# A grouped convolution whose three tap blocks are multiplied last to first

## The reference

```python
x = x + conv1d(x, W0, taps=9, groups=4, pad=4) + ctx0 + side     # layer 0
x = x + einsum(agg_w1[b], x) + agg_b1                            # layer 1, one 128x128 matrix per batch
x = x + einsum(agg_w2[b], x) + agg_b2                            # layer 2, likewise
x = x + conv1d(x, W3, taps=9, groups=4, pad=4) + ctx3 + side     # layer 3
# agg_w[b] = sum over 8 experts of softmax(mlp(cond[b])) * expert weight
```

## Time and profile before

| | |
|---|---|
| profiled execution | 2548.97 us |
| its span | 2547.1 us |
| PE busy | 2520.7 us, 99% |
| PEld busy | 2062.1 us, 81% |
| ACT busy | 2252.2 us, 88% |
| DVE busy | 1995.5 us, 78% |
| DMA engines, queue 1 | 87.3% |
| granted TensorE clock, mean | 0.996 |

### The profile page before, as it was taken

The page is one execution under the profiler, slowest core; times in us unless marked ns, Lnnn a source line. Parts: engine busy times, 40 slices in busy tenths (PEclk is TensorE's granted clock), DMA queues, the critical chain, the costliest instruction groups (busy, mean ns, idle before and its releaser), DMA issues.

```text
span 2547.1 us, 43755 instructions
## 1 busy us (share of the span) xinstructions
PE 2520.7 (99%) x11068; PEld 2062.1 (81%) x11068; DVE 1995.5 (78%) x5032; ACT 2252.2 (88%) x2449; POOL 16.0 (1%) x27
## 2 busy tenths in 40 slices
PE   7999999999999999999999999999999999999997
PEld 6888888888888888888888888888888888888886
DVE  8777787778777878787877778777877787888784
ACT  6889998999899989998998899899989998998895
POOL 2000000000000000000000000000000000000000
PEclk9999999999999999999999999999999999999999
DMA  7889889888888888899889888988888888888986
GB/s 257 318 332 331 328 324 334 329 328 325 332 328 327 329 333 326 325 333 328 329 326 333 330 329 324 333 329 329 325 333 329 327 327 333 325 326 333 329 312 235
DMA packets 334986, 825.56 MB, mean 324 GB/s; under 512 B 37370, under 2 KB 39426, under 8 KB 302210
## 3 DMA queue, kind: packets, MB, share of 16 engines
q1 hardware_dynamic: 332736, 823.94, 87.3%
q10 hardware_dynamic: 2242, 1.53, 0.2%
HBM read 137.97 MB, written 134.23 MB: 107 GB/s over the span
## 4 chain that ended last, share of the span: by engine, by line
PE 97%; DVE 1%; DMA 1%; ACT 1%; SPq 0%; issue 0%; ACTq 0%; DVEq 0%
PE pair L930 82%; PE quad L980 14%; PE pair L970 1%; DVE partial L754 0%; DMA x_ch<-x_ph 0%; DMA mix<-att_saved 0%; ACT x_ch L473 0%; ACT x_out L525 0%; DVE operands L790 0%; DMA x_ph<-in_small 0%; DVE operands L787 0%; DMA x_ph<-x_ch 0%; SPq L318 0%; SPq L370 0%; DVE operands L714 0%
## 5 line engine op out<-in xcount | busy, mean ns | idle before, releaser
L930 PE MATMUL pair<-operands 128*128 128x512 f32 x9216 | 2157.3, 393 | 3.4 <-DVE operands L805 1.8
L930 PEld LDWEIGHTS pair<-operands 128*128 128x128 f32 x9216 | 1722.6, 188 | 385.8 <-DVE operands L805 2.2
L473 ACT COPY x_ch<-x_in 128x1088 f32<-128x1088 f32 x255 | 556.9, 2184 | 0.0
L787 DVE CAST operands<-x_ch 128x512 fp32r<-128x512 f32 x512 | 205.4, 422 | 437.4 <-DMA x_ch<-x_ph 437.4
L525 ACT COPY x_out<-x_ch 128x1024 f32<-128x1024 f32 x252 | 524.2, 2080 | 0.2 <-DMA x_ch<-x_ph 0.2
L542 ACT ACTIVATE x_ph<-pair,bias_now 128x512 f32<-128x512 f32 x508 | 354.8, 699 | 187.6 <-PE pair L930 187.6
L533 ACT ACTIVATE x_ph<-pair,bias_now 128x512 f32<-128x512 f32 x512 | 357.5, 698 | 77.5 <-PE pair L930 69.7
L754 DVE SCALAR_TENSOR_TENSOR partial<-expert,mix,partial 128x128 f32<-128x128 f32 x1536 | 416.4, 349 | 0.0
L980 PE MATMUL quad<-operands 128*128 128x512 f32 x1536 | 372.9, 392 | 2.4 <-DVE operands L790 2.4
L805 DVE TENSOR_TENSOR operands<-x_ph,operands 128x542 fp32r<-128x542 f32 x512 | 357.7, 721 | 0.0
L980 PEld LDWEIGHTS quad<-operands 128*128 128x128 f32 x1536 | 289.7, 189 | 66.6 <-issue 3.1
(11 more groups left out here) (77 smaller groups left out, 214.2 us busy)
## 6 DMA issues: line engine op xcount, KB each, us to landing
x_ch<-x_ph SPq DMA_DIRECT2D x1024, 256.0 KB, 3.0
x_ph<-x_ch SPq DMA_DIRECT2D x512, 272.0 KB, 2.9
x_ph<-x_ch SPq DMA_DIRECT2D x512, 271.0 KB, 2.6
x_in<-in_x SPq DMA_DIRECT2D x128, 1024.0 KB, 5.7
out<-x_out SPq DMA_DIRECT2D x128, 1024.0 KB, 4.3
x_out<-in_W SPq DMA_DIRECT2D x8, 144.0 KB, 4.4
expert<-in_e ACTq DMA_DIRECT2D x2, 512.0 KB, 8.5
mix<-att_saved SPq DMA_DIRECT2D x2, 512.0 KB, 6.8
```

The source lines that it names most:

```text
L473: nc.scalar.copy(to, of).then_inc(x_cut, 1)
L930: mm = nc.tensor.matmul(conv_bank[g % 2], w[l][:, m, g, :], x[:, g, m * SEG:m * SEG + N], start=(m == 0 and x is hi and w is w_hi), stop=( ...
```

## The change

Within a group of nine matmuls the block index runs 2, 1, 0 in place of 0, 1, 2. The flags that open and close the accumulation move along with it. The three products inside a block keep their order, the groups keep theirs, and no wait, semaphore, load, copy or DMA is touched. The list of instructions of each engine shows the same rows before and after; only the columns of `operands` that the matmuls of L930 name differ.

```diff
             def conv(l, g, hi, lo, done):
-                for m in range(BLK):
+                for m in reversed(range(BLK)):
                     for w, x in ((w_hi, hi), (w_hi, lo), (w_lo, hi)):
                         mm = nc.tensor.matmul(conv_bank[g % 2], w[l][:, m, g, :], x[:, g, m * SEG:m * SEG + N],
-                                              start=(m == 0 and x is hi and w is w_hi),
-                                              stop=(m == BLK - 1 and w is w_lo))
+                                              start=(m == BLK - 1 and x is hi and w is w_hi),
+                                              stop=(m == 0 and w is w_lo))
                 mm.then_inc(done, 1)
```

## The result

The changed kernel takes 2560.93 us (median of 5 runs, 2560.0 to 2564.1), the kernel before 2548.66 us (5 runs, 2548.07 to 2548.96). The ratio is 1.0052, with a 95% interval of 1.0037 to 1.0066: slower, by 12.3 us. The profiled execution has a span of 2559.1 us, 12.0 us more than before.

A forecast was written before the change was run, and what follows sets the result against it. TensorE's 9216 convolution matmuls were taken as the bound (PE busy 99%). Four terms of 0 against the profiled 2548.97 us, with the median of runs 0.31 us lower, gave 2548.7 us; range 2530 to 2566 us.

The forecast's parts named there:

- The likeliest case: Whole kernel: no difference beyond 0.2%, 5 us either way, 2544 to 2554 us; chance 0.38.
- both rivals: Convolution groups: faster, 2533 us or in full 2518 us, chance 0.29; slower, 2559 us, chance 0.33.
- The slower rival: Convolution groups: TensorE never regains its even pace; 0.01 us per group, +10 us, 2559 us; chance 0.33.
- Part (1): All engines: no instruction or wait removed, added or moved; cost 0.
- part (2): Accumulation's opening and closing flags move to the blocks now first and last; cost 0.
- The pot of 0.03 us per group: Convolution groups: extra over the middle layers' pace, 2.07 against 2.04 us, 31 us of the run.
- part (4): Between groups the step goes from 0 to 64 columns, into the middle layers it becomes +32; both taken as 0.
- part (3): Inside each group two steps of +16 become -16; taken as 0, bounds -31 to +41 us.
- the +32 into the middle layers: Step from convolution into middle layers, 128 times in place of 0; taken as 0.
- The bound of 4 us: Upper price of the +32 steps into the middle layers, 128 of them at 0.03 us each.
- The rival's mechanism: Slower case: a third step, of 64, at each group's end keeps reads disturbed throughout the group; +10 us, chance 0.33.
- the sign that it named: Slower case, numbers 0 to 2 of each group: numbers 0 and 1 lose their 389 ns records.

The follow-up runs named there:

- lo_first: Kernel before, same block order, but each block takes low weights by high x first, then high by high, high by low; 2549.08 us, ratio 0.9999.
- steps: Probe with single's rows, weights and omissions: slice and weights step together once per group, before matmul number 3, by +16, -16 or +32; 2535.53 us, one run.
- w_shift64: Kernel before with all weights of both convolutions laid 64 columns further on, order and steps unchanged; 2549.22 us, ratio 1.000.
- w_shift16: Kernel before with all weights of both convolutions laid 16 columns further on, order and steps unchanged; 2569.66 us, ratio 1.0084.
- scan: Probe without steps inside a group: one slice, same weights everywhere, no low part, weights laid 0 to 56 columns further on across eight groups; 2570.21 us, one run.
- single: Probe with scan's rows and omissions, all at column 0 modulo 64 except slice or weights displaced 16 columns around matmul number 4; 2547.06 us, one run.
- lo_prev: As lo_first, with low weights laid to match, modulo 64, the slice of the block ahead in time; 2548.75 us, ratio 0.9999 against the kernel before.
- w_shift48: Kernel before with all weights of both convolutions laid 48 columns further on; 2552.98 us, ratio 1.0018.

## Why the prediction was right, and where it was wrong

The time lies inside the range, 2530 to 2566 us. The likeliest case, no difference, did not come in, and the forecast itself, 2548.7 us, missed by 12 us; the range holds the result because it reached into both rivals. The slower rival did come in, with 2559 us forecast and 2560.93 measured, and that its number is so close is in part luck. It charged 0.01 us to each of 1024 groups; a steady group pays 0.007 us, and the difference is made up at two places that it did not name.

**Right.** TensorE sets the end: its 95 ns per batch, times 125, are the 12 us. Part (1), no wait and no work added, holds: L930 waits 4.0 us against 3.4. The flags of part (2) cost nothing that shows; lo_first moved them too, from one product to another, and left the time as it was. The pot of 0.03 us per group was the right place to look. The step of 64 between groups, part (4), costs nothing that shows: the changed kernel runs 42, 54, 36, 46, 42 across it, and the kernel steps ends its +16 with the same 42, 54, 36, 46, 42 where there is no further step at all. That w_shift64 leaves the time as it was fits.

**Wrong: part (3), "a step of -16 has the same size as one of +16, falls on the same places of the group, and there are as many", priced at 0.** Size and number do not make the price. The two steps of -16 cost 88 cycles a group where the two of +16 cost 72, 7 ns more; over 1024 groups that is 7 us of the 12. What the runs put in its place is an interplay: the price of a step depends on whether the aftermath of the one before it is over. A step of +16 alone costs 100 cycles and one of -16 alone 28 (steps). In both kernels a second step follows three matmuls after the first. For +16 it cuts a long aftermath short: 72 for two, less than the 100 for one. For -16 it comes one matmul too early: the changed kernel runs 30, 38, 46, 42 as in steps, but the second step falls beside that 42, and what follows is 42, 54, 36, 46, 42 (60 cycles) and not a second 30, 38, 46, 42 (28). The kernel steps has both in it: its steps of -16 in group 3 of conv1 and group 1 of conv4 are 18 matmuls apart, and each costs 28. So with the even pace reached in between a second step costs 28 cycles, and three matmuls behind the first, inside its aftermath, it costs 60. This is measured in two kernels that differ in more than the spacing (steps leaves out part of the weights and of the slices); spacings between 3 and 18 were not run, and why the aftermath has this form stays open.

**Wrong: the +32 into the middle layers, taken at 0.** It costs 17 ns per batch in the middle layers and 7 ns in the last distance of conv4, together 3 us. The bound of 4 us held. From an even pace it costs 10 ns (steps); here it meets the disturbance of conv4's last block.

**The rest**, some 2 us, is for the most part group 1 of conv1. Before, the restart behind the expert matrices happened to bring that group to an even pace (32, 32, 30 at its start, 2.060 us); in the changed kernel it does not (54, 36, 48, 2.087 us). That is 27 ns per batch, 7 of them the steady price of two steps, 20 on top. Groups 0 to 2 of conv4, often disturbed already before, take back a little of it.

**The rival's mechanism** was half right. Number 0 of group 1 did lose its 389 ns (397 now), number 1 kept it, though its distance grew from 32 to 36 cycles; in groups 2 and 3 numbers 0 and 1 had 395 and 393 ns in both kernels, so the sign that it named could show in one group only. The disturbance does leave no even distance in the whole group. But it named the third step, of 64, as the reason, and that one is free.

**The rule weighed in the prediction**, a fixed 216 ns and loads that take nothing from the running matmul ("TensorE: Matmul & The Clock Gate", the Trainium skill), would give 0 for every one of these kernels. The page's section "Back-to-back issue gap" gives the formula for isolated matmuls; for a stream of pairs of load and matmul it has about 131 ns at 512 columns, which the prediction left out. No run here comes near that: an even stream starts one every 226.7 ns. The runs differ by 21 us through placement alone (w_shift16 against before), so here the measurement decides against the rule.

## What to carry to other kernels

When TensorE is the bound and streams 512 columns of 4-byte operands at full clock, look at the start columns of weights and slices modulo 64: keep each matmul's weights and slice at the same value, and step as seldom as the layout allows. The price of a step is not a constant to add up; it depends on how many matmuls lie between it and the next, so a new order must be read from start-to-start distances over a whole period, not from one step. This was shown with fp32r operands and one weight load per matmul only. Records of single matmuls that differ by a few ns in a fixed sequence are a signal, and 7 ns in 2070 repeated 1024 times is 7 us.

## What the runs showed of the hardware

- An even stream of 128x512 fp32r matmuls, each with its own weight load, starts one every 226.7 ns at full clock; constant distances other than 0 between weights and slice raise that to 229 (distance 48) or 232 to 234 ns (scan).
- The effect has a period of 64 columns, 256 bytes: weights laid 64 columns further on leave the time at 2549.22 us, 16 columns cost 21 us (w_shift64, w_shift16), and a distance of 32 is slow (232 ns, scan).
- One step or one displaced operand is felt over 2 to 11 matmuls, with the same sequence in every batch (single, steps). Several of the longer aftermaths end alike, with 54, 36, 46, 42 and then 32 (steps +16; single, slice or weights moved alone; the steady groups of before and after). A mechanism that keeps such a memory was not found; how loads and slices meet inside TensorE or SBUF stays open. It is open too why before, lo_prev and w_shift48, with three different sequences, all come to 2.070 us a group.
